# The scales of the FFN quantisation move from VectorE to GpSimd in a fused decoder block

## What is computed

```python
x = _layernorm(x + rwkv(x))              # time mix, log-domain recurrence over 256 steps, sigmoid gate, Wo
x = _layernorm(x + xattn(x, ctx_1024))   # 16 heads of 16, rms norm and rope on q and k, softmax over 77 keys
x = _layernorm(x + ffn(x))               # the part that the change touches

def _weight_quant(w):
    scale = 1.0 / jnp.clip(jnp.mean(jnp.abs(w)), 1e-05)
    return jnp.clip(jnp.round(w * scale), -1.0, 1.0) / scale
def _act_quant(x):
    scale = 127.0 / jnp.clip(jnp.max(jnp.abs(x), axis=-1, keepdims=True), 1e-05)
    return jnp.clip(jnp.round(x * scale), -128.0, 127.0) / scale
def _bitlinear(x, w):
    return jnp.einsum('bsi,oi->bso', _act_quant(x), _weight_quant(w))
gate = jax.nn.silu(_bitlinear(x, w_gate))            # w_gate, w_up: 1024 x 256
up = _bitlinear(x, w_up)
return _bitlinear(gate * up, w_down)                 # w_down: 256 x 1024
```

## Time and profile before

| | |
|---|---|
| median of 3 runs | 1168.77 us |
| the profiled execution, its own time | 1178.08 us |
| its span, first to last instruction | 1176.4 us |
| mean granted TensorE clock | 0.943 |
| TensorE matmul busy | 1033.3 us (88%) |
| VectorE busy | 976.7 us (83%) |
| ScalarE busy | 882.5 us (75%) |
| GpSimd busy | 681.3 us (58%) |

### The profile page before, as it was taken

How to read it: one execution, slowest core, us unless ns; L and a number is a source line. 1 busy time by engine, 2 the same in 40 slices (tenths; PEclk the granted TensorE clock), 3 DMA queues, 4 the chain that set the end, 5 groups by cost and what they waited for, 6 DMA issues and landing times. The chain is left out here.

```text
span 1176.4 us, 21274 instructions
## 1 busy us (share of the span) xinstructions
PE 1033.3 (88%) x6434; PEld 766.2 (65%) x6466; DVE 976.7 (83%) x2345; ACT 882.5 (75%) x1590; POOL 681.3 (58%) x1209
## 2 busy tenths in 40 slices
PE   3558999999999999999998999999999999998774
PEld 2335666777766676777776676677776766667551
DVE  2765899899899999899898999999899899985443
ACT  4254678788887888888887788888888777886645
POOL 4355666666666666566566766666566666654300
PEclk7777999999999999999999999999999999996986
DMA  7001011111011111111011111111001111100000
GB/s 222 18 4 24 23 24 32 33 34 31 6 33 34 33 33 32 33 33 33 6 31 34 33 33 32 33 33 34 22 15 34 34 32 33 32 15 13 12 10 18
DMA packets 83110, 36.91 MB, mean 31 GB/s; under 512 B 54837, under 2 KB 82485, under 8 KB 82997
## 3 DMA queue, kind: packets, MB, share of 16 engines
q1 hardware_dynamic: 82997, 35.56, 11.4%
HBM read 24.62 MB, written 8.39 MB: 28 GB/s over the span
## 5 line engine op out<-in xcount | busy, mean ns | idle before, releaser
L506 POOL TENSOR_TENSOR mneg<-zeros,mv 128x2 f32<-128x2 f32 x96 | 18.7, 195 | 260.9 <-DVE mv L1127 260.9
L957 PEld LDWEIGHTS pb<-v_blk,p_t 128*128 128x128 f32 (+1 forms) x1280 | 151.3, 195 | 9.7 <-ACT p_t L716 9.7
L957 PE MATMUL pb<-v_blk,p_t 128*128 128x51 f32 (+2 forms) x1280 | 154.6, 278 | 2.1 <-ACT p_t L716 2.1
L687 ACT ACTIVATE gate_silu<-pg,gate_scale 128x512 f32<-128x512 f32 x128 | 87.9, 687 | 57.8 <-PE pg L1001 56.3
L716 ACT ACTIVATE p_t<-pb 128x512 f32<-128x512 f32 x160 | 90.9, 589 | 43.5 <-PE pb L937 25.2
L1310 DVE TENSOR_REDUCE m_pad<-pb 128x4 bf16<-128x308 f32 x256 | 114.2, 468 | 11.1 <-PE pb L912 11.0
L1249 DVE TENSOR_TENSOR hid<-gate_silu,pu 128x512 f32<-128x512 f32 x128 | 87.7, 685 | 24.4 <-PE pu L1001 21.2
L629 ACT ACT_TABLE_LOAD x74 | 94.9, 1283 | 1.3
L1135 DVE SCALAR_TENSOR_TENSOR mix<-dx,vec,x_t 128x256 f32<-128x256 f32 x192 | 86.9, 511 | 5.4 <-POOL dx L569 5.4
L862 PE MATMUL pk<-mix,w_sb 128*128 128x256 f32 x256 | 73.9, 417 | 19.7 <-DVE mix L1135 8.0
L576 POOL TENSOR_TENSOR den_cur<-e_cur,bb 128x512 f32<-128x512 f32 x32 | 37.8, 1180 | 89.4 <-DVE bb L1191 88.7
(11 more groups left out here) (180 smaller groups left out, 2984.6 us busy)
## 6 DMA issues: line engine op xcount, KB each, us to landing
x_t<-xt SPq DMA_DIRECT2D x32, 256.0 KB, 2.7
x_tok<-x SPq DMA_DIRECT2D x32, 256.0 KB, 3.1
out<-outb SPq DMA_DIRECT2D x32, 256.0 KB, 3.4
ctx_t<-ctxt SPq DMA_DIRECT2D x32, 77.0 KB, 3.1
w_sb<-wts SPq DMA_DIRECT2D x8, 256.0 KB, 7.2
v_blk<-v_sb SPq DMA_DIRECT2D x128, 9.6 KB
hid<-wg SPq DMA_DIRECT2D x1, 1024.0 KB, 7.3
hid_int<-wu SPq DMA_DIRECT2D x1, 1024.0 KB, 9.4
```

Source lines behind the costliest of these rows:

```text
L687: sc.activation(gate_silu[:, u % 2, :], pg[:, :], ACT.Silu, scale=gate_scale[:, u // 2:u // 2 + 1]).then_inc(sil_ready, 1)
L957: last = mm(pb[j][:, c0:c0 + NHEAD[n] * VW], p_t[0:k, q, s, j * P:(j + 1) * P], v_blk[p][0:k, g, n, 0:NHEAD[n] * VW], start=q == 0 and s == 0,
```

## The change

Three multiplications leave VectorE and become two GpSimd tasks, with a semaphore each. `ffn_scales` (gate and up scale) stands in GpSimd's list behind `ln_scale(0)` and before `den_cur`; `ffn_down_scale` stands behind `newton_t` and before `ln_scale(1)`. The readers wait on the new semaphores, and VectorE waits before it overwrites what the new tasks read. The order of all other tasks is kept.

```diff
+            def ffn_scales(b):
+                pool.wait_ge(amax_ready, 3 * b + 2)
+                wait(pool, sil_ready, 4 * b)
+                wait(pool, hscale_ready, 3 * b)
+                pool.tensor_tensor(out=gate_scale[:, :], in0=amax_step[:, :], in1=wmean[:, 0:1].broadcast_to([P, J]), op=ALU.mult)
+                pool.tensor_tensor(out=up_scale[:, :], in0=amax_step[:, :], in1=wmean[:, 1:2].broadcast_to([P, J]), op=ALU.mult
+                                   ).then_inc(scales_ready, 1)
+            def ffn_down_scale(b):
+                pool.wait_ge(hscale_ready, 3 * b + 1)
+                wait(pool, raw_ready[2], 2 * b)
+                pool.tensor_tensor(out=down_scale[:, :], in0=hmax_clip[:, :], in1=wd127[:, 2:3].broadcast_to([P, J]), op=ALU.mult
+                                   ).then_inc(dscale_ready, 1)
...
                 if s[2]: rwkv_newton(s[2][0])
+                if s[5]: ffn_down_scale(s[5][0])
                 if s[4]: ln_scale(1, s[4][0])
                 if s[2]: ln_scale(0, s[2][0])
+                if s[4]: ffn_scales(s[4][0])
                 if s[1]: rwkv_den(s[1][0])
...
             def gate(b, u):
                 act.wait_ge(gate_ready, 4 * b + u + 1)
+                if u == 0:
+                    act.wait_ge(scales_ready, b + 1)
...
                 elif n == 1:
                     dve.wait_ge(amax_ready, 3 * b + 1)
+                    wait(dve, scales_ready, b)
                     v.tensor_scalar(amax_step[:, :], ...)
                 elif n == 2:
                     dve.wait_ge(amax_ready, 3 * b + 2)
-                    wait(dve, sil_ready, 4 * b)
-                    v.tensor_scalar(gate_scale[:, :], amax_step[:, :], wmean[:, 0:1], None, ALU.mult)
-                    v.tensor_scalar(up_scale[:, :], amax_step[:, :], wmean[:, 1:2], None, ALU.mult)
                     v.reciprocal(x_scale[:, :], amax_step[:, :]).then_inc(amax_ready, 1)
...
                 if n == 0:
                     dve.wait_ge(hmax_ready, 2 * b + 2)
+                    dve.wait_ge(scales_ready, b + 1)
+                    wait(dve, dscale_ready, b)
...
                 elif n == 1:
                     dve.wait_ge(hscale_ready, 3 * b + 1)
-                    v.tensor_scalar(down_scale[:, :], hmax_clip[:, :], wd127[:, 2:3], None, ALU.mult)
                     v.reciprocal(hmax_rec[:, :], hmax_clip[:, :]).then_inc(hscale_ready, 1)
...
             def ffn_residual(b, j, p):
                 dve.wait_ge(down_ready, 2 * b + j + 1)
+                if j == 0:
+                    dve.wait_ge(dscale_ready, b + 1)
```

More of the change, by code:

```diff
@@ L287, in build @@
         hscale_ready = sem("hscale_ready")
+        scales_ready = sem("scales_ready")
+        dscale_ready = sem("dscale_ready")
         hu_ready = sem("hu_ready")
```

## The result

| | before | after |
|---|---|---|
| median, 10 runs each | 1173.38 us (1167.14 to 1176.24) | 1157.84 us (1156.24 to 1163.91) |
| profiled execution, own time / span | 1178.08 / 1176.4 us | 1156.24 / 1154.4 us |
| ratio after/before | | 0.9882 [0.9864, 0.9900] |

The changed kernel is faster by 1.18%, 13.8 us (11.7 to 16). The prediction was 1162.3 us with a range of 1156 to 1172; its sum was 6.4 us, so the gain was underestimated by half. Measured again in another series the same kernel took 1159.88 us beside 1171.23 us, ratio 0.9909 [0.9874, 0.9945], 10.7 us; the two intervals overlap, and the gain lies somewhere between 10 and 15 us.

The account below looks back on a forecast made before the run. A ring between VectorE and TensorE was taken as the bound, no engine being plainly full. 5.8 + 2.6 - 0.3 - 1.7 = 6.4 us off 1168.77 gave 1162.4, rounded to 1162.3 us; range 1156 to 1172.

Parts of the forecast that it names:

- rival 3: Whole steady step: more than the sum, each 0.39 us arrives, TensorE's side following fully; 1156.5 us, chance 0.06.
- the narrower forecast: Whole kernel's time: the prediction's own case, 1158.5 to 1165.5 us, chance 0.53.
- the two paths: Gate and up scale directly behind amax_step, 0.26 us a step; down_scale through kms and newton_t to d_old, up to 0.13 us.
- The ring: Steady loop: VectorE without a gap from second rden to the maxima, then TensorE back to rden; VectorE work removed there shortens it.
- the second path: Without down_scale on VectorE, GpSimd's kms ends earlier, then newton_t, then VectorE's d_old; up to 0.13 us a step.
- gate and up scale: VectorE behind amax_step: removal advances what follows by 0.26 us; TensorE's side follows by 0.18, 5.8 us over 32 batches.
- down_scale: VectorE before rden: removal ends kms and d_old earlier by 0.13 us in 20 steps, 2.6 us; bounds 0 and 4.2.
- The waits: VectorE's four more semaphore waits, less one lost, all for things long done: cost 0.3 us, 1 us at most.
- the common access: New GpSimd operations beside x_int and d_old: VectorE and GpSimd hold each other up; cost 1.7 us, bounds nothing and 19.
- Rival 1: Time given away again at rden's wait, ScalarE's table load or TensorE's own work; 1167.5 us, chance 0.27.
- Rival 2: Shared access decides: new GpSimd operations go ahead of x_int and d_old, 0.6 us a step; 1175 us, slower, chance 0.14.
- The mix row: Profile row, four mix beside three GpSimd operations, 1.68 us against 1.63 alone; basis for 0.02 us an operation.

Follow-up runs that it names:

- e5: Kernel before with two useless 128x2 copies of down_scale added on VectorE ahead of scan aa; 1157.87 us, ratio 0.9868 to before.
- e9: Changed kernel with two useless 128x2 operations added on VectorE between den and the reciprocal hmax_rec; 1150.71 us, ratio 0.9824 to before.
- e10: Kernel before with one useless 128x2 operation added on VectorE behind down_scale, ahead of the reciprocal and aa; 1155.71 us, ratio 0.9860.
- e2: Changed kernel with gate and up scale back on VectorE, only down_scale on GpSimd; 1163.03 us, ratio 0.9935 to before.
- e3: Changed kernel without the three multiplications and their waits, tiles holding a constant, output not the reference's; 1159.94 us, ratio 0.9900 to before.
- e7: Changed kernel with VectorE's order altered so that aa runs early, ahead of den and hmax; 1150.55 us, ratio 0.9824 to before.
- e11: e7 with pp moved in front of the last scale step instead of behind it; 1147.22 us, ratio 0.9799 to before.
- e1: Changed kernel with down_scale back on VectorE, only gate and up scale on GpSimd; 1163.94 us, ratio 0.9931 to before.
- e4: Changed kernel measured and profiled once more, nothing altered; 1159.88 us, ratio 0.9909 to before.
- e6: Kernel before with two useless 128x2 operations added on VectorE behind aa, ahead of hid_scale; 1173.79 us, ratio 1.0025 to before.
- e8: Kernel before, run and profiled once more, nothing altered; 1169.48 us in one run.

## Why the prediction was right, and where its sizes were off

- **The forecast.** It was right by its range, whose lower end was set by rival 3; of the narrower forecast, 1158.5 to 1165.5, the time is outside. The direction and the two paths were right; every term of the sum was off to the same side.
- **The ring, right.** Both ways by which work was to leave it were found as described, with the instructions named: x_scale straight behind amax_step, kms and d_old each shorter by 0.12 to 0.13 us. The step is 32.22 to 32.255 us; I had written 32.3 to 32.4. The picture of kms behind the second path held for the change and not beyond it: "held until VectorE's row of operations is through" is true with one or two short operations between den and aa, and with three or four kms is let in behind den (e5, e9, e10). That the change stays on the one side of this border was not foreseen; it is luck.
- **gate and up scale, "I take 0.18 x 32 = 5.8 us", too small.** The edit measures 0.24 us a step, 0.24 x 32 = 7.7 us, nearly the whole 0.26. I had capped it by the 0.15 us that TensorE waits for rneg. The x1 transposes moved by 2.75 - 2.51 = 0.24 us: the product queue ahead of them and ScalarE's x1 let them in that early. A wait in a row says how long the engine stood, not how far its work can move once the releaser is earlier; what bounds it next had to be read from the next input's time.
- **down_scale, "I take 20 steps x 0.13 = 2.6 us", too small.** e2 has it in all the steps: 0.13 x 32 = 4.2 us, my upper bound. The 10 waits of raw, from which I took 12 steps off, do not hide it, since the product hangs on the same kms and moves too; I had said so in the sentence before and then discounted for it all the same.
- **The waits (0.3 us) and the common access (1.7 us), both 0.** e3 without any of it has the same step within 0.03 us, 1 us in all.
- **The sum** by the measured sizes is 7.7 + 4.2 = 11.9 us; it lies between the two measured differences, 10.7 and 13.8 us. That it comes so near is in part chance: the whole change measures 0.335 and 0.37 us in the median step, 10.7 to 11.8 us over 32, and fewer of the longer steps add 3.0 us in the first pair of profiles and 1.9 in the second. The sum had no term for these. I had named them only as a sign (the forecast falls if their number changes by more than three); it changed by three. Without the two discounts and the two costs the sum of the prediction was 12.5 us. That was its third rival ("each 0.39 us arrives"), to which I gave 0.06.
- **Rival 1 (given away again) is refuted**: the waits for m_pad are unchanged, none is new, and the step is not 32.55 us. **Rival 2 (the shared access decides) is refuted** for these three operations: e3 against after. The mix row, four operations with three short GpSimd ones beside them, was the right one to go by. The Trainium skill (SBUF — State Buffer, "Who interferes with whom") states that of two operations that contend the one that starts first has the shared ports for its whole instruction and the other fully blocks. newton_t with d_old agrees with it (805.29 before 805.60). The rest does not follow from it, if the recorded starts are the order: kms is recorded 0.09 us before den and is held all the same, over den, the short operations and both scans (798.46 before 798.55), hid_scale in e7 is recorded 0.07 us before num and is the one held, and gate_scale, recorded 0.03 us behind the start of x_int, takes 0.20 us, no longer than mneg, where it would have been blocked if x_int is of the kind that contends. So the prediction's sentence that by that rule "d_old's 1.37 us and kms's 2.15 us are explained" holds for d_old and is not shown for kms.
- **The base.** I worked from 1168.77 us, the median of three runs; over ten it is 1173.38. The predicted 1162.3 would have been 1167 from there: the absolute value came near by an error in the base that offsets part of the error in the sum.
- **Open.** The number of longer steps among the 28 varies from kernel to kernel (0 to 8), each costs 0.85 to 1.3 us, and I have no edit that governs it. Most of them show a granted clock of 0.95 (six of before's seven, three of after's four). The number repeats in two profiles of before (seven, seven) and of after (four, four), which speaks against plain chance; but e3, with the same median step as after, has seven. e7 and e11 have none, so some of their gain may lie there.

## What to carry to other kernels

Work moved from the engine on the ring to one with time to spare brings its start-to-start distance, here 0.13 us for a 128x2 operation, and it may bring it twice over: directly, and by ending sooner the row of operations that keeps the other engine out. Where an operation in a profile takes several times its usual duration (kms: 77x16 elements, 2.15 us, ended with a neighbour's scan; 0.22 us in the first and the last steps, where nothing holds it), look at what ends with it and try another order there first. One more operation in before was worth 0.38 us a step (e10), as much as the three that were moved, and the move with two such operations added 0.62 us (e9). When a term is capped by a recorded wait, look up when the next input is there before the cap is used.

## What the runs showed of the hardware

- Adding work made the kernel faster: one 128x2 operation more on VectorE between den and aa (three operations there instead of two) lets GpSimd's kms end 1.29 us earlier, with 0.86 us instead of 2.15, and the kernel takes 0.986 of its time. One or two operations between: held until the scans end (before, after, e1, e2, e3, e4, e6, e8). Three or four: not held (e5, e9, e10). Whether the number counts or the time is open, since no kernel here changes one without the other: from den's end to aa's start it is 0.00 us (after) and 0.13 (before) where kms is held, 0.26 (e9, e10) and 0.39 (e5) where it is not.
- Short GpSimd operations of 128x2 beside VectorE's tensor_scalar of 128x256 cost VectorE nothing that shows (0.62 and 0.63 us) and take 0.20 to 0.24 us themselves instead of 0.195. Long ones do cost: the mix of the earlier trace rows that stands for one alone is the first of four, and another of the four takes 1.50 us beside GpSimd's qab of 128x512, which runs from 628.87 to 630.37.
- The reverse holds for a long one: VectorE's hid_scale, 128x2, is recorded with 1.26 us in e7 beside GpSimd's num, 128x512, and 0.13 us in after.
- Waits on semaphores set long before cost VectorE nothing measurable: four more in each step, together with the three GpSimd operations, 32.22 to 32.255 us against 32.23 without both (e3).
